# Attention over four images, one core: value work moved behind k and q, the small load moved to another queue

## The chip, the core and the metric

One core of a Trainium2 chip runs the whole kernel. It has a matrix engine (TensorE, in the profile PE, its weight loads PEld), a vector engine (VectorE, DVE), a scalar engine (ScalarE, ACT), GpSimd (POOL) and a queue engine (SyncE, SP), which here only issues loads and stores. Each engine runs its own instructions in order and waits on semaphores for the others. The metric is the device time of one execution in microseconds; the median over the runs counts.

## The reference

```python
q = jnp.einsum('oc,bcn->bon', Wq, xf) + bq[None, :, None]     # 32 x 1024 per image
k = jnp.einsum('oc,bcn->bon', Wk, xf) + bk[None, :, None]     # 32 x 1024
v = jnp.einsum('oc,bcn->bon', Wv, xf) + bv[None, :, None]     # 256 x 1024
scores = jnp.einsum('bqi,bqj->bij', q, k)                     # 1024 x 1024, no scaling
attn = jax.nn.softmax(scores, axis=-1)
out = jnp.einsum('bcj,bij->bci', v, attn)
return out.reshape(B, Cc, W, H) + x
```

There are four images of 256 channels and 32 x 32 = 1024 pixels, all in fp32.

## The kernel before

Every fp32 operand of a matrix product is held as two parts that TensorE takes at its fast rate: a *high* part (the number rounded to the type fp32r) and a *low* part (the rest). A product is then three matmuls: high by high, high by low, low by high. "Cutting" makes a high part, "splitting" the low part. The work of the other engines is mostly this, next to softmax.

An image runs through these steps. k and q are projected from the image (two halves of 512 pixels). Scores are made eight times 128 rows by 1024 columns; for each, VectorE takes the row maximum (`row_max`, L667) and ScalarE sums the exponentials of the row (`sum_exp`, L504). Then the scores are made once more, transposed and already shifted by the maximum (`scores_t`, L996: 128 keys by 512 pixels), ScalarE takes their exponential (`exp`, L539 and L542), which VectorE or POOL splits, and TensorE weighs the values with it (`weigh_v`, L1009 and L1015) into the banks `acc`. Values are eight tiles of 128 pixels by 256 channels (`v_tile`, L849: six matmuls each); two tiles share a bank, and a bank is cut by ScalarE or VectorE (`first_cut_v`) and split by VectorE (`split_v`, L715).

From image 1 on, a table (FRONT) lays the next image's steps between the weighting of the current one. Image 0 has nothing to hide behind: its beginning is an order written out by hand for each engine, and that is what the change rewrites. In it, the small load (`small_sb`: weights of k and q, biases) is issued by ScalarE, two loads of image 0 (one for each half of its channels), the value weights `wv` and image 1 by SP. TensorE runs twenty matmuls on zeros (`keep_busy`, L1076) until k and q can be projected (`first_project_qk`, L876 to L881). Of the 1024 pixels, q is put in three parts: pixels 0 to 255 (part 0), 256 to 511 (part 1) and the rest. For scores, `k_a` holds k high, k high again and k low, `q_a` holds a copy of q high (POOL's `put_q_dup`), q low (`put_q_lo`) and q high.

For image 0, only the first four scores (`first_scores` 0 to 3) are needed before the transposed scores of its first half; their row maxima are turned into rows by a small product with the identity (`first_rows`, L970), which ScalarE copies into `q_b` (`put_first_rows`, L514). Scores 3 use the bank of scores 0 again, so they wait until ScalarE has summed those (`rowsum_ready`). The banks of value tiles 0 to 3 are in `slot1`, those of tiles 4 to 7 in `slot0`, which scores 1 use before them. The weighting of key tile 0 waits for the split of the values it uses (`weigh_ready`, `v_split`).

## Time and profile before

| | us |
|---|---|
| median of 3 runs | 163.89 (163.86 to 164.11) |
| the profiled execution | 163.81 |
| its span in the trace | 162.0 |
| busy: TensorE, VectorE, ScalarE, POOL | 157.5, 133.9, 109.2, 60.0 |

The profile is of one execution. Its page gives busy times, the chain of work that ended last (followed back from the end, at each step to what released it), the costliest groups of instructions and the loads. The timeline shows single instructions with their start, their duration, and in brackets how long the engine had idled before and what ended that. A duration runs to the end of an instruction, and the next may start a little earlier, so of two equal ones the distance of the starts can be shorter than one duration. TensorE's ends are modelled. "Stretches" are tables of busy time between two times. The granted clock there is TensorE's as a share of full speed.

### The profile page before, as it was taken

The numbers are of one execution on the slowest core, as the hardware profiler recorded it, in microseconds if no ns is written. First come the engines' busy times: TensorE is split into PE (matmuls) and PEld (weight loads), VectorE is DVE, ScalarE is ACT, GpSimd is POOL, SyncE is SP. The second block draws the span as 40 slices with busy tenths as digits, with TensorE's granted clock in tenths as the row PEclk, the third lists the DMA queues.
The fourth block names the chain that finished last, engine by engine and source line by source line (L and its number), as shares of the span: only waits on it lengthen the run. The fifth ranks groups of instructions, "written<-read, shape, count | busy, mean of one in ns | idle before, by whom it ended". The sixth has DMA issues, their size and how long they took to land.

```text
span 162.0 us, 2456 instructions
## 1 busy us (share of the span) xinstructions
PE 157.5 (97%) x788; PEld 132.3 (82%) x788; DVE 133.9 (83%) x215; ACT 109.2 (67%) x200; POOL 60.0 (37%) x68
## 2 busy tenths in 40 slices
PE   7999999999999999999999999999999999999993
PEld 5677887798888887798888897788888898888882
DVE  1899998888988989997989989895989779846952
ACT  3679887969999545827999646736896655756400
POOL 4479946256222316348443300342333300124500
PEclk9999999999999999999999999999999999999999
DMA  4576672152103030162711130162320330003003
GB/s 161 187 299 166 243 235 89 31 151 63 55 0 97 1 129 2 37 144 67 268 39 49 54 129 0 37 146 67 121 61 1 97 129 0 0 5 129 0 0 130
DMA packets 7780, 14.67 MB, mean 91 GB/s; under 512 B 1504, under 2 KB 2072, under 8 KB 7768
## 3 DMA queue, kind: packets, MB, share of 16 engines
q1 hardware_dynamic: 6728, 13.46, 25.4%
q0 software_dynamic: 608, 0.80, 2.2%
q10 hardware_dynamic: 432, 0.26, 0.5%
q8 instruction: 6, 0.10, 0.3%
q14 instruction: 6, 0.05, 0.1%
HBM read 4.79 MB, written 4.20 MB: 55 GB/s over the span
## 4 chain that ended last, share of the span: by engine, by line
PE 90%; DMA 2%; ACT 2%; DVE 2%; issue 1%; DVEq 0%
PE acc L1009 32%; PE acc L1015 16%; PE slot L849 11%; PE st L996 9%; PE slot L909 7%; PE slot L1009 5%; DMA small_sb<-small 2%; PE slot L1015 2%; ACT dump L504 2%; PE slot L861 2%; PE slot L866 2%; PE slot L935 1%; DVE negmax L667 1%; PE slot L881 1%; DVE x_lo L632 0%
## 5 line engine op out<-in xcount | busy, mean ns | idle before, releaser
L402 POOL TENSOR_TENSOR w_lo<-w_full,w_hi 128x512 fp32r<-128x512 f32 x21 | 28.0, 1338 | 46.6 <-ACT w_full L542 25.4
L1009 PE MATMUL acc<-w_hi,v_hi 128*128 128x512 f32 x112 | 44.3, 395 | 0.0
L1009 PE MATMUL acc<-w_hi,v_lo 128*128 128x512 f32 x112 | 44.1, 394 | 0.0
L542 ACT ACTIVATE w_full<-st 128x512 f32<-128x512 f32 x62 | 36.8, 594 | 7.6 <-PE st L996 7.5
L504 ACT ACTIVATE dump<-slot,negmax 128x1024 f32<-128x1024 f32 x29 | 32.5, 1119 | 10.5 <-DVE negmax L667 10.1
L667 DVE TENSOR_REDUCE negmax<-slot 128x1 f32<-128x1024 f32 x29 | 35.2, 1217 | 2.7 <-PE slot L909 2.7
L1015 PE MATMUL acc<-w_lo,v_hi 128*128 128x512 f32 x112 | 37.4, 396 | 0.0
L734 DVE TENSOR_TENSOR w_lo<-w_full,w_hi 128x512 fp32r<-128x512 f32 x43 | 30.7, 719 | 3.6 <-issue 0.5
L1009 PEld LDWEIGHTS acc<-w_hi,v_hi 128*128 128x128 f32 x112 | 21.1, 189 | 5.0 <-issue 0.2
L1009 PEld LDWEIGHTS acc<-w_hi,v_lo 128*128 128x128 f32 x112 | 21.2, 189 | 4.8
L1015 PEld LDWEIGHTS acc<-w_lo,v_hi 128*128 128x128 f32 x112 | 21.0, 188 | 4.8
L996 PE MATMUL st<-q_b,k_b 98*128 98x512 f32 x62 | 24.5, 398 | 0.1
L725 DVE CAST w_hi<-w_full 128x512 fp32r<-128x512 f32 x40 | 19.5, 489 | 3.0 <-ACT w_full L542 1.5
L539 ACT ACTIVATE w_hi<-st 128x512 fp32r<-128x512 f32 x24 | 14.3, 594 | 6.2 <-PE st L996 6.0
L849 PE MATMUL slot<-wv_hi,x_hi 128*128 128x256 f32 x62 | 17.4, 281 | 0.4 <-ACT dump L504 0.4
L849 PE MATMUL slot<-wv_lo,x_hi 128*128 128x256 f32 x62 | 17.4, 281 | 0.0
L849 PE MATMUL slot<-wv_hi,x_lo 128*128 128x256 f32 x62 | 17.3, 280 | 0.0
L909 PE MATMUL slot<-k_a,q_a 96*128 96x512 f32 x48 | 15.2, 397 | 0.0
L531 ACT ACTIVATE v_hi<-slot 128x512 fp32r<-128x512 f32 x12 | 7.2, 599 | 11.8 <-PE slot L849 11.8
L265 POOL DMA_DIRECT2D q_b<-shift_rows x7 | 4.2, 602 | 29.5 <-DVE shift_rows L706 27.0
L715 DVE TENSOR_TENSOR v_lo<-slot,v_hi 128x512 fp32r<-128x512 f32 x16 | 11.0, 690 | 3.8 <-ACT v_hi L531 3.7
L909 PEld LDWEIGHTS slot<-k_a,q_a 96*128 96x128 f32 x48 | 13.0, 310 | 1.1
(102 smaller groups left out, 225.2 us busy)
## 6 DMA issues: line engine op xcount, KB each, us to landing
out<-x_sb SPq DMA_DIRECT2D x7, 512.0 KB, 2.8
x_sb<-x SPq DMA_DIRECT2D x3, 1024.0 KB, 5.1
k_b<-k_a SPq DMA_DIRECT2D x8, 192.0 KB, 2.6
q_b<-q_a SPq DMA_DIRECT2D x8, 192.0 KB, 2.6
x_sb<-x SPq DMA_DIRECT2D x2, 512.0 KB, 4.2
k_a<-qk_parts SPq DMA_DIRECT2D x12, 64.0 KB, 2.0
q_a<-qk_parts SPq DMA_DIRECT2D x12, 64.0 KB, 2.2
k_a<-qk_parts POOLq DMA_DIRECT2D x6, 64.0 KB, 2.2
```

The source lines that it names most:

```text
L402: nc.gpsimd.tensor_tensor(w_lo[:, r, :], w_full[:, r, :], w_hi[:, r, :].bitcast(fp32), ALU.subtract).then_inc(w_split_pool, 1)
L504: nc.scalar.activation(dump[:, t % 2, :], s_home(b, t), ACT.Exp, bias=negmax[:, t:t + 1], accum_out=rowsum[:, t:t + 1]).then_inc(rowsum_re ...
L539: nc.scalar.activation(w_hi[:, r, :], st_home(n), ACT.Exp).then_inc(w_cut_act, 1)
L542: nc.scalar.activation(w_full[:, r, :], st_home(n), ACT.Exp).then_inc(exp_done, 1)
L667: nc.vector.tensor_reduce(out=negmax[:, t:t + 1], in_=s_home(b, t), op=ALU.max, axis=AX.X, negate=True).then_inc(negmax_ready, 1)
L725: nc.vector.tensor_copy(w_hi[:, r, :], w_full[:, r, :]).then_inc(w_cut_dve, 1)
L734: nc.vector.tensor_tensor(w_lo[:, r, :], w_full[:, r, :], w_hi[:, r, :].bitcast(fp32), ALU.subtract).then_inc(w_split_dve, 1)
L849: last = nc.tensor.matmul(dst, lhs, rhs, start=(i == 0), stop=(i == len(terms) - 1))
L909: last = nc.tensor.matmul(s_home(b, t)[:, cols(h)], pixels(b, t), k_a[0:K_A, cols(h)], start=True, stop=True)
L996: nc.tensor.matmul(st_home(n), k_b[0:K_B, j * P:(j + 1) * P], q_b[0:K_B, cols(h)], start=True, stop=True).then_inc(st_ready, 1)
L1009: nc.tensor.matmul(dst, v[:, b % 2, j, c * P:(c + 1) * P], w_hi[:, n % RING, part], start=(j == 0 and v is v_hi), stop=False)
L1015: return nc.tensor.matmul(dst, v_hi[:, b % 2, j, c * P:(c + 1) * P], w_lo[:, n % RING, part], start=False, stop=(j == JT - 1))
```

## The change

- SP issues the small load, between the two loads of image 0, instead of ScalarE.
- VectorE splits the first quarter of image 0 (`x_lo`) before it makes the low part of the weights, and TensorE's first projection takes its three products in that order.
- q's first part is put by ScalarE (`put_q_hi(0)`), not VectorE; ScalarE alternates k and q and casts the value weights (`wv_hi`) only behind them. VectorE makes k low before q low.
- POOL copies the first q part before it builds the weight pairs for later images, the second before it splits the value weights; its cuts and splits of image 1 have other places among its first splits of weights.
- TensorE runs 18 warming matmuls, not 20, and 4 more behind the projection; first scores 0 come ahead of all values. Value tile 0 is made in two pieces (`first_v_high`, `first_v_low`), around scores 1 and 2; tile 1 follows, then scores 3, then tiles 2 and 3.
- ScalarE casts the first bank of values behind `put_first_rows`, not ahead of the sums. VectorE splits bank 1 before bank 0, and cuts bank 2 between them; the first weighting waits for two splits instead of one.

TensorE after the projection of k and q. Before, the rows are the last products of value tile 1 (L849), then scores 0, 1 and 2 (L935), then value tile 2:

```order
L849 MATMUL slot<-wv_hi,x_hi 128x256
L849 MATMUL slot<-wv_lo,x_hi 128x256
L849 MATMUL slot<-wv_hi,x_lo 128x256
L935 MATMUL acc<-k_a,q_a 128x512 [waits q_dup_put,q_lo_put,k_lo_put]
L935 MATMUL acc<-k_a,q_a 128x512 [waits k_lo_put]
L935 MATMUL slot<-k_a,q_a 128x512 [waits q_lo_put]
L935 MATMUL slot<-k_a,q_a 128x512
L935 MATMUL st<-k_a,q_a 128x512 [waits q_dup_put]
L935 MATMUL st<-k_a,q_a 128x512
L849 MATMUL slot<-wv_hi,x_hi 128x256 [waits q2_full_put]
```

and now (L1086 warming, L941 scores, L958 and L964 the two pieces of value tile 0):

```order
L1086 MATMUL st<-idle 128x256 x4
L941 MATMUL acc<-k_a,q_a 128x512 [waits q_dup_put,q_lo_put,k_lo_put]
L941 MATMUL acc<-k_a,q_a 128x512 [waits k_lo_put]
L958 MATMUL slot<-wv_hi,x_hi 128x256 [waits wv_cut]
L958 MATMUL slot<-wv_hi,x_lo 128x256
L958 MATMUL slot<-wv_hi,x_hi 128x256
L958 MATMUL slot<-wv_hi,x_lo 128x256
L941 MATMUL slot<-k_a,q_a 128x512 [waits q_lo_put]
L941 MATMUL slot<-k_a,q_a 128x512
L941 MATMUL st<-k_a,q_a 128x512 [waits q_dup_put]
L941 MATMUL st<-k_a,q_a 128x512
L964 MATMUL slot<-wv_lo,x_hi 128x256 [waits wv_split]
```

Value tiles 0 and 1 stood ahead of scores 0; now tile 0 lies around scores 1 and 2, and tile 1 follows the last row.

TensorE around scores 3 (into `acc`, waiting for the first sum). Before, the last products of value tile 3 stand ahead of it and tile 4 behind it:

```order
L849 MATMUL slot<-wv_hi,x_hi 128x256
L849 MATMUL slot<-wv_lo,x_hi 128x256
L849 MATMUL slot<-wv_hi,x_lo 128x256
L935 MATMUL acc<-k_a,q_a 128x512 [waits rowsum_ready]
L935 MATMUL acc<-k_a,q_a 128x512
L849 MATMUL slot<-wv_hi,x_hi 128x256 [waits rowsum_ready]
```

and now, where the row that waits for `q2_full_put` begins value tile 2:

```order
L850 MATMUL slot<-wv_hi,x_hi 128x256
L850 MATMUL slot<-wv_lo,x_hi 128x256
L850 MATMUL slot<-wv_hi,x_lo 128x256
L941 MATMUL acc<-k_a,q_a 128x512 [waits rowsum_ready]
L941 MATMUL acc<-k_a,q_a 128x512
L850 MATMUL slot<-wv_hi,x_hi 128x256 [waits q2_full_put]
L850 MATMUL slot<-wv_lo,x_hi 128x256
```

Two tiles (2 and 3) moved from before scores 3 to behind it; between scores 3 and the shift rows there are now four tiles, and there were two.

ScalarE from the cast of the value weights (L569) to the first exponential (L539), before:

```order
L569 ACTIVATE wv_hi<-wv 128x512 [waits wv_in]
L554 ACTIVATE k_a<-slot,small_sb 64x512 [waits qk_ready,small_in]
L554 ACTIVATE k_a<-slot,small_sb 64x512 [waits qk_ready]
L560 ACTIVATE q_a<-slot,small_sb 32x256 [waits q_lo_put]
L565 ACTIVATE qk_rest<-slot,small_sb 32x512 [waits qk_ready]
L523 ACTIVATE v_hi<-slot 128x512 [waits v_ready]
L504 ACTIVATE dump,rowsum<-acc,negmax 128x1024 [waits negmax_ready]
L504 ACTIVATE dump,rowsum<-slot,negmax 128x1024 [waits negmax_ready]
L504 ACTIVATE dump,rowsum<-st,negmax 128x1024 [waits rowsum_ready,negmax_ready]
L504 ACTIVATE dump,rowsum<-acc,negmax 128x1024 [waits rowsum_ready,negmax_ready]
L514 ACTIVATE q_b<-st 2x512 [waits row_ready]
L539 ACTIVATE w_hi<-st 128x512 [waits st_ready]
```

and now (L578 the value weights, L526 the first values):

```order
L557 ACTIVATE k_a<-slot,small_sb 64x512 [waits qk_ready,small_in]
L564 ACTIVATE q_a<-slot,small_sb 32x256
L557 ACTIVATE k_a<-slot,small_sb 64x512 [waits qk_ready]
L564 ACTIVATE q_a<-slot,small_sb 32x256 [waits q_lo_put]
L578 ACTIVATE wv_hi<-wv 128x512 [waits wv_in]
L569 ACTIVATE qk_rest<-slot,small_sb 32x512 [waits qk_ready]
L507 ACTIVATE dump,rowsum<-acc,negmax 128x1024 [waits negmax_ready]
L507 ACTIVATE dump,rowsum<-slot,negmax 128x1024 [waits negmax_ready]
L507 ACTIVATE dump,rowsum<-st,negmax 128x1024 [waits rowsum_ready,negmax_ready]
L507 ACTIVATE dump,rowsum<-acc,negmax 128x1024 [waits rowsum_ready,negmax_ready]
L517 ACTIVATE q_b<-st 2x512 [waits row_ready]
L526 ACTIVATE v_hi<-slot 128x512 [waits v_ready]
```

The value weights moved from ahead of k to behind q, the first values from ahead of the sums to behind the copy of the shift rows; q's first part came in.

The diff, cut to its core:

```diff
 (SP)
             for c in range(CT):
                 sp.dma_start(x_sb[:, 0, c, :], x_v[0, :, c, :]).then_inc(x0_in[c], DMA)
+                if c == 0:
+                    sp.dma_start(small_sb[:, :], small).then_inc(small_in, DMA)
 (POOL)
+            put_q_dup(0)
+            pool.wait_ge(q_dup_put, 1)
             for half, (parts, made) in enumerate(((wqk_hi, wqk_cut), (wqk_lo, wqk_split))):
...
             pool.wait_ge(pair_made, 2)
+            put_q_dup(1)
+            pool.wait_ge(q_dup_put, 2)
             pool.wait_ge(wv_cut, 1)
             nc.gpsimd.tensor_tensor(wv_lo[:, :, :], wv[:, :, :], wv_hi[:, :, :].bitcast(fp32),
                                     ALU.subtract).then_inc(wv_split, 1)
             pool.wait_ge(wv_split, 1)
-            put_q_dup(0)
-            pool.wait_ge(q_dup_put, 1)
-            put_q_dup(1)
-            pool.wait_ge(q_dup_put, 2)
...
+            pool.wait_ge(shift_ready, 1)
             cut_x1(1)
             split_x1(1)
             pool.wait_ge(x1_split, 2)
-            pool.wait_ge(shift_ready, 1)
             cut_x1(2)
+            pool.wait_ge(w_split_dve, SPLIT_COUNT[0])
             split_x1(2)
             pool.wait_ge(x1_split, 3)
+            split_w(1)
             cut_x1(3)
             pool.wait_ge(x1_cut, 4)
-            split_w(1)
 (ScalarE)
-            act.dma_start(small_sb[:, :], small).then_inc(small_in, DMA)
...
+            act.wait_ge(small_in, DMA)
+            put_k_hi(0)
+            put_q_hi(0)
+            put_k_hi(1)
+            put_q_hi(1)
             act.wait_ge(wv_in, DMA)
             nc.scalar.activation(wv_hi[:, :, :], wv[:, :, :], ACT.Copy).then_inc(wv_cut, 1)
-            act.wait_ge(small_in, DMA)
-            put_k_hi(0)
-            put_k_hi(1)
-            put_q_hi()
             put_q2_full()
-            first_cut_v(0)
             for t in range(TH):
                 sum_exp(0, t)
             put_first_rows()
+            first_cut_v(0)
             exp(0)
 (VectorE)
-            dve.wait_ge(qk_ready, 1)
-            nc.vector.tensor_scalar(out=q_a[2 * CQK:3 * CQK, Q_PARTS[0]], in0=q_home(0), ...
+            put_k_lo(0)
             put_q_lo(0)
-            put_k_lo(0)
             put_k_lo(1)
             put_q_lo(1)
             for t in range(TH):
                 row_max(0, t)
             first_shifts()
-            split_v(0, 0)
             first_cut_v(1)
             split_v(0, 1)
+            first_cut_v(2)
+            split_v(0, 0)
             invert_sums()
-            first_cut_v(2)
             split_v(0, 2)
 (TensorE)
+            def first_v_high():
+                pe.wait_ge(wv_cut, 1)
+                for c in range(CT):
+                    for xs in (x_hi, x_lo):
+                        nc.tensor.matmul(v_home(0, 0)[:, 0:C], xs[:, 0, c, 0:P], wv_hi[:, c, :], ...
+            def first_v_low():
+                pe.wait_ge(wv_split, 1)
+                for c in range(CT):
+                    nc.tensor.matmul(v_home(0, 0)[:, 0:C], x_hi[:, 0, c, 0:P], wv_lo[:, c, :], ...
...
-                    pe.wait_ge(v_split, 4 * b + 1 + j // VT)
+                    pe.wait_ge(v_split, 4 * b + 1 + j // VT if b + j else 2)
...
-            keep_busy(20, QUARTER)
+            keep_busy(18, QUARTER)
             for i in range(4):
                 first_project_qk(i)
-            pe.wait_ge(wv_cut, 1)
-            v_tile(0, 0)
-            v_tile(0, 1)
+            keep_busy(4, QUARTER)
             first_scores(0)
+            first_v_high()
             first_scores(1)
             first_scores(2)
+            first_v_low()
+            v_tile(0, 1)
+            first_scores(3)
             pe.wait_ge(q2_full_put, 1)
             v_tile(0, 2)
             v_tile(0, 3)
-            first_scores(3)
```

## Rows read from the trace of the kernel before

**Rows 1.** The page: busy time by engine; the last chain by engine.

```profile
PE 157.5 (97%) x788; PEld 132.3 (82%) x788; DVE 133.9 (83%) x215; ACT 109.2 (67%) x200; POOL 60.0 (37%) x68
...
PE 90%; DMA 2%; ACT 2%; DVE 2%; issue 1%; DVEq 0%
```

**Rows 2.** The chain of waits from 0 to 25 us: start, us, what.

```profile
0.75 3.94 DMA small_sb<-small
...
9.78 0.70 PE slot L849 x6
...
11.17 1.24 DVE negmax L667
...
17.05 0.59 ACT q_b L514
```

**Rows 3.** Timeline, 0 to 8 us: start, us, engine, line, operation, [idle before <- releaser].

```profile
0.74 0.86 SPq L278 DMA_DIRECT2D x_sb<-x  x2
...
4.50 1.15 ACT L490 ACTIVATE x_hi<-x_sb 128x512 fp32r<-128x512 f32 x2 [2.04 <-DMA x_sb<-x]
4.71 0.29 DVE L624 CAST wqk_hi<-small_sb 128x256 fp32r<-128x256 f32 x1 [3.43 <-DMA small_sb<-small]
5.04 0.43 DVE L626 TENSOR_TENSOR wqk_lo<-small_sb,wqk_hi 128x256 fp32r<-128x256 f32 x1
...
5.38 2.68 DVE L632 TENSOR_TENSOR x_lo<-x_sb,x_hi 128x512 fp32r<-128x512 f32 x4
...
7.72 0.39 PE L881 MATMUL slot<-x_lo,wqk_hi 128*128 128x512 f32 x1
```

**Rows 4.** Stretches: from:to, us, busy by engine, granted clock, load share, GB/s.

```profile
2.00:3.00 1.00, 1.00 (x7) 0.69 (x6) 0.00 (x0) 0.46 (x1) 0.84 (x1) 1.00 0.54 176
3.00:4.00 1.00, 1.00 (x6) 0.71 (x5) 0.00 (x0) 0.00 (x0) 0.00 (x0) 1.00 1.06 410
...
24.00:160.00 136.00, 135.22 (x675) 114.92 (x673) 114.84 (x185) 91.74 (x171) 43.92 (x44) 1.00 0.22 69
```

**Rows 5.** Timeline, 8 to 11 us: VectorE and ScalarE on k and q.

```profile
8.15 0.48 DVE L769 TENSOR_SCALAR q_a<-slot,small_sb 32x256 fp32r<-32x256 f32 x1
...
8.21 1.31 ACT L554 ACTIVATE k_a<-slot,small_sb 64x512 fp32r<-64x512 f32 x2 [0.72 <-PE slot L881]
...
9.18 1.40 DVE L642 SCALAR_TENSOR_TENSOR k_a<-slot,small_sb,k_a 32x512 fp32r<-32x512 f32 x2
```

**Rows 6.** Timeline, 13 to 17 us: TensorE's scores 3 and shift rows.

```profile
13.69 0.74 PE L935 MATMUL acc<-k_a,q_a 96*128 96x512 f32 x2
...
16.41 0.40 PE L970 MATMUL st<-eye_r,shift_parts 128*2 128x128 f32 x4
```

**Rows 7.** Timeline, 10 to 24 us: casts and splits of values, exponentials, weighting.

```profile
10.62 0.60 ACT L523 ACTIVATE v_hi<-slot 128x512 fp32r<-128x512 f32 x1
...
18.23 0.60 ACT L539 ACTIVATE w_hi<-st 128x512 fp32r<-128x512 f32 x1 [0.59 <-PE st L996]
...
18.92 0.69 DVE L715 TENSOR_TENSOR v_lo<-slot,v_hi 128x512 fp32r<-128x512 f32 x1
...
18.97 0.47 PE L1009 MATMUL acc<-w_hi,v_hi 128*128 128x512 f32 x1
...
21.98 1.11 ACT L504 ACTIVATE dump<-slot,negmax 128x1024 f32<-128x1024 f32 x1
...
23.24 0.54 PEld L935 LDWEIGHTS slot<-k_a,q_a 96*128 96x128 f32 x2 [0.27 <-ACT dump L504]
```

**Rows 8.** Timeline, 7 to 22 us: POOL's subtractions.

```profile
7.64 1.58 POOL L424 TENSOR_TENSOR wv_lo<-wv,wv_hi 128x512 fp32r<-128x512 f32 x1 [1.34 <-ACT wv_hi L569]
...
12.09 1.28 POOL L384 TENSOR_TENSOR q_a<-qk_rest,q_a 32x512 fp32r<-32x512 f32 x1
...
20.92 1.29 POOL L402 TENSOR_TENSOR w_lo<-w_full,w_hi 128x512 fp32r<-128x512 f32 x1 [0.23 <-ACT w_full L542]
```

**Rows 9.** Timeline of TensorE alone, 3.5 to 4.5 us: warming matmuls.

```profile
3.17 1.70 PE L1076 MATMUL st<-idle 128*128 128x256 bf16 x7
```

More of the change, by code:

```diff
@@ L766, in finish @@
                                                scalar=bv_sb[:, c:c + 1], in1=x_sb[:, b, c, cols(h)], op0=ALU.add, op1=ALU.add).then_inc(acc_read, 1)
-            dve.wait_ge(qk_ready, 1)
-            nc.vector.tensor_scalar(out=q_a[2 * CQK:3 * CQK, Q_PARTS[0]], in0=q_home(0),
-                                    scalar1=bias[2 * CQK:3 * CQK, 0:1], scalar2=None,
-                                    op0=ALU.add).then_inc(q_hi_put, 1)
+            put_k_lo(0)
             put_q_lo(0)
-            put_k_lo(0)
             put_k_lo(1)
@@ L877, in first_project_qk @@
                 if i == 0:
+                    pe.wait_ge(x0_split, 1)
+                    nc.tensor.matmul(dst, wqk_hi[:, c, :], x_lo[:, 0, c, part], start=False, stop=False)
                     pe.wait_ge(wqk_split, 1)
+                    nc.tensor.matmul(dst, wqk_lo[:, c, :], x_hi[:, 0, c, part], start=False, stop=False)
+                    return
                 nc.tensor.matmul(dst, wqk_lo[:, c, :], x_hi[:, 0, c, part], start=False, stop=False)
```

27 lines of the change are left out of this document (12 added, 15 removed).

## The prediction

> **What bounds the kernel now.** I read the page first: TensorE is busy for 97% of the span and carries 90% of the chain that ended last [rows 1]. The stretch from 24 to 160 us is 136.0 us long and TensorE is busy in 135.2 of them [rows 4]. Nothing is won or given back there: what the first 24 us gain or lose reaches the end whole. The change touches only those 24 us, so the chain of that stretch is the next view [rows 2]. It is no TensorE chain at first: the small load lands at 4.69, weights and image 0 are cut, k and q are made, VectorE takes the first row maximum at 11.17, ScalarE runs four sums of exponentials, copies the shift rows at 17.05, and only then come transposed scores, exponentials and the weighting (18.97 in [rows 7]). Values and POOL's splits have room beside this chain; the question for each edit is whether it shortens the chain or eats that room.
>
> **The change part by part.** *Loads and weight cut.* The small load moves behind the first half of image 0 on SP's queue. Before, ScalarE starts to cut that half at 4.50, VectorE the weights at 4.71 [rows 3]. The load is 128 x 132 x 4 = 68 KB, 0.16 us at the 410 GB/s of the stretch from 3 to 4 us [rows 4]; so much sooner may the half land. VectorE's instructions stay (0.29, 0.43, four x low of 2.68 / 4 = 0.67), only the first x low goes ahead of the weights' low part. With the old landings it starts at 4.50 + 0.62 = 5.12 (one cut is 0.62, since two take 1.15 overlapped), and the third ends at 5.12 + 0.67 + 0.43 + 2 x 0.67 = 7.56; before it ended at about 7.4 and TensorE, slightly behind, ended the first half of k and q at 7.72 + 0.39 = 8.11 [rows 3]. After it can end near 8.1, with the 0.16 nearer to 7.95. I take **-0.1**. No row shows a small load behind another on SP's queue, so the bounds are wide: +0.2 and -1.0 (rivals below). The two dropped warming matmuls end before the weights are there and cost nothing.
>
> The Trainium skill (Trainium Kernel Development and Optimization, Key Constraints) says that loads issued by SP, ScalarE and GpSimd run on the same engines and interleave, and that issuing from several only saves issue time. By that rule the move buys no bandwidth, and the small load waits for SP's issue of the half ahead of it; that is the second rival, and the trace of before can't decide it.
>
> *k and q.* Before, VectorE made q high, q low, k low, k low: from 8.15 to 10.58 (the last row, 9.18 + 1.40) [rows 5]. Now ScalarE makes q high and VectorE waits for k high first: 8.21 + 0.68 (half of the pair's 1.31, and a little) = 8.89, then k low 0.66 (spacing within that pair of 1.40), q low 0.48 (as long as q high), k low 0.74 with small gaps: 10.83. That is +0.25, and with the -0.1 above **+0.15** for the second half of the first scores and so for the first row maximum (11.17 becomes 11.32). ScalarE's part hides: its second k high ends at about 9.9, before VectorE wants it at 10.1.
>
> *Values behind k and q.* Value weights are cast at about 10.5 to 11.1 instead of 6.9, and TensorE's queue holds the first value products between scores 0 and scores 1. Scores 1 then end near 12.2, and the second row maximum wants them at 11.32 + 1.13 = 12.45: covered by 0.2. POOL does the weight pairs and both q copies first, then the values' low part, which took 1.58 at 7.64 but of which a like subtraction took 1.28 at 12.09 [rows 8]. It ends between 12.4 and 13.1, and TensorE does tile 1 of the values behind it, 0.7 us [rows 2]. Scores 3 can't start before the first sum has freed its bank, 13.69 + 0.15 = 13.84 [rows 6], so a low part that ends by 12.9 costs nothing; I take 1.28 and no cost, and 0.2 as the upper bound.
>
> The Trainium skill (GPSIMD Engine Reference, 1. Specifications) says that POOL shares its SBUF interfaces with VectorE and contends with VectorE's instructions of two SBUF inputs. The rows agree: 1.58 stands beside the x low subtractions, 1.28 beside row maxima out of PSUM. By the rule the low part takes 1.28 in its new place and the sum stays; with 1.58 it would be 0 to 0.2 higher.
>
> *Scores 3.* Here is the price. Before, value tiles 2 and 3 ran ahead of scores 3, in its wait. Now tile 1 stands there and tiles 2 and 3 behind it. From 13.84 TensorE has scores 3 (two matmuls, 0.47), four value tiles at 0.70 [rows 2] and the shift rows: these start at 13.84 + 0.47 + 2.80 = 17.11 instead of 16.41, and take 0.40 [rows 6], so ScalarE may copy at 17.5. ScalarE's own sums would let it copy at 17.05 + 0.15 = 17.20. Before, TensorE was 17.05 - 16.81 = 0.24 early; now it is last, by 0.3. The copy comes **+0.5** late, of which 0.15 is the k and q step.
>
> *First values in ScalarE's wait.* The copy takes 0.59, the transposed scores follow, and before ScalarE idled 0.59 in front of the first exponential [rows 7]; the cast of the first values is 0.60, so it fits and costs at most 0.05. But VectorE can split these values only then: copy done at 18.1, cast done at 18.75, split (0.69) done at 19.45 [rows 7]. The weighting now waits for two splits; it would start at 18.97 + 0.5 = 19.47 anyway. A tie, and no cost.
>
> *VectorE behind that split.* The third split, 18.92 before [rows 7], comes after the reciprocal at 19.5, **+0.6** instead of +0.5; behind it stand, in the old order, the first weights' low part, the last split and the row maximum of scores 4. The exponential of scores 4 at 21.98 goes to 22.6 with it, and TensorE already waited 0.27 us for the end of that one at 23.24 [rows 7]. So the next point at which TensorE waited moves by 0.6 and not by 0.5. POOL's first low part of weights (20.92, 1.29) [rows 8] now stands behind a third x low and ends near 23.4; TensorE wants it at about 23.3. That wait lies inside the 0.6, with 0.3 as the upper bound.
>
> **Sum.** -0.1 + 0.25 + 0.35 (scores 3) + 0.1 (VectorE behind the late split) = **+0.6 us**. The profiled execution took 163.81, so 164.41; it stands 0.08 under the median of 163.89, so the forecast is 164.5. With the bounds of the unknown costs (-0.3 for better landings, +0.4 for POOL and for a small load that lands later) the forecast's own range is 164.2 to 164.9.
>
> **Rivals.** *Earlier loads, and faster.* In the stretch from 2 to 3 us the load engines moved 176 GB/s against 410 in the next [rows 4]. Were the fault ScalarE's load among the first rows, image 0 could land up to (410 - 176) / 410 = 0.57 sooner, and at the most 1.0 with a shorter way from last byte to wait. A gain of 0.6 is needed to balance, 0.95 to come out faster by over 0.2%. At 1.0 in place of my 0.1 the time is 164.5 - 0.9 = 163.6. For it speaks the slow stretch; against it that 410 is reached with both queues at work, and that the second half's landing at about 5.8 would have to move too. Faster 0.07; the milder form, 0.3 to 0.95 sooner, gives 163.7 to 164.2: 0.15.
>
> *Small load later.* Two issues of SP take 0.86 [rows 3]. If the small load lands later by one of them, at 5.1, VectorE starts its chain there: 5.1 + 0.3 + 0.67 + 0.43 + 1.34 = 7.85, k and q end near 8.4 in place of 8.0, and the first weights cost 0.3 to 0.4: 164.8. The long landing of before (3.9 us for 68 KB) speaks for a load that waits its turn. 0.09.
>
> *TensorE falls to its lower clock.* The warming matmuls of 256 columns come at seven in 1.70 us [rows 9], some 0.21 apart once the last one's own tail is taken off, the level of 1.2 GHz; a value tile's six in 0.70 [rows 2], 0.117 apart, that of 2.4. The granted clock's column reads 1.00 even in the slow stretch [rows 4], so the spacing tells it. Between the projection and scores 3 the new order leaves holes (about 0.9, 0.5 and 0.3 us) where before value tiles stood. If the clock fell there, five tiles would take 3.5 us more, of which at most 0.5 is covered; with a quick return about half, 166 to 167.5. Against it: four new warming matmuls, and no hole above 1 us. 0.05.
>
> The Trainium skill (TensorE: Matmul & The Clock Gate, Part 1) says that the low clock is the default and that recent activity releases it; no run so far shows a fall in this kernel.
>
> **Chances.** Forecast 0.64, later small load 0.09, low clock 0.05: slower by over 0.2% (0.33 us, about what a measurement of this kernel can tell from no change) 0.78. Within it 0.15, faster 0.07. The range takes in the milder loads and the later small load, and leaves most of the clock and of the faster case out: 163.8 to 165.1.
>
> **What would show it.** In the profile after: first row maximum near 11.3; shift rows (TensorE into st, 128 columns) at 17.1, and ScalarE's copy released by them and not by its own last sum; VectorE idle for some 0.5 us ahead of the split of the first values; the weighting at 19.5; TensorE's wait for the exponential of scores 4 ending near 23.9. It is wrong if the first row maximum comes before 10.8 (loads), if POOL's low part of the value weights ends after 13.2, or if value tiles take over 1 us each (clock).

## The result

The changed kernel takes 165.94 us at the median of 6 runs (165.49 to 166.80), the kernel before 163.88 (163.71 to 164.11): ratio 1.0129, 95% interval 1.011 to 1.0148, so **slower by 2.06 us**, where the prediction had +0.6 and a range up to 165.1. The profiled execution of after took 165.96 with a span of 164.2 (before 163.81 and 162.0). Two single executions of later kernels, 312.65 (e13) and 221.19 (e17), lie far above all others, and the ratios, unlike the medians, leave them out. The page of after, busy times and last chain, against [rows 1]:

```profile
PE 158.8 (97%) x790; PEld 132.5 (81%) x790; DVE 135.0 (82%) x214; ACT 109.8 (67%) x201; POOL 58.5 (36%) x68
...
PE 96%; DVE 2%; ACT 0%; issue 0%; DVEq 0%; ACTq 0%
```

The chain is now 96% TensorE's (90% before): behind the first scores nearly nothing else stands between two steps. The busy times say little; where the time went is read in the order of time. Timeline of after, 0 to 8 us, against [rows 3]; last a row of before:

```profile
1.19 0.42 SPq L281 DMA_DIRECT2D small_sb<-small  x1
1.65 0.43 SPq L278 DMA_DIRECT2D x_sb<-x  x1
...
4.19 1.15 ACT L493 ACTIVATE x_hi<-x_sb 128x512 fp32r<-128x512 f32 x2 [2.16 <-DMA x_sb<-x]
4.37 0.29 DVE L629 CAST wqk_hi<-small_sb 128x256 fp32r<-128x256 f32 x1 [3.09 <-DMA small_sb<-small]
...
6.92 1.16 ACT L493 ACTIVATE x_hi<-x_sb 128x512 fp32r<-128x512 f32 x2 [1.58 <-DMA x_sb<-x]
```

```profile
5.82 1.15 ACT L490 ACTIVATE x_hi<-x_sb 128x512 fp32r<-128x512 f32 x2 [0.17 <-DMA x_sb<-x]
```

The first half of image 0 and the weights land 0.3 earlier, as the prediction's -0.1 wanted. The second half lands at 6.92, where it was 5.82, and ScalarE stands idle for 1.58. Stretches of after (from:to, us, busy by engine, granted clock, load share, GB/s):

```profile
3.00:4.00 1.00, 1.00 (x6) 0.71 (x5) 0.00 (x0) 0.00 (x0) 0.00 (x0) 1.00 0.87 247
4.00:5.00 1.00, 1.00 (x7) 0.52 (x4) 0.44 (x2) 0.81 (x2) 0.00 (x0) 1.00 0.75 148
```

Before, the stretch from 3 to 4 moved 410 GB/s [rows 4], the next 408; now the load engines are busy for 0.87 and 0.75 of two stretches and move 247 and 148. Then k, q and the first scores, 8 to 13 us, against [rows 5]:

```profile
8.94 0.68 ACT L557 ACTIVATE k_a<-slot,small_sb 64x512 fp32r<-64x512 f32 x1 [0.86 <-PE slot L887]
...
9.64 0.46 ACT L564 ACTIVATE q_a<-slot,small_sb 32x256 fp32r<-32x256 f32 x1
...
11.01 0.47 PE L941 MATMUL acc<-k_a,q_a 96*128 96x512 f32 x1 [1.02 <-DVE q_a L653]
...
12.27 1.23 DVE L672 TENSOR_REDUCE negmax<-acc 128x1 f32<-128x1024 f32 x1
```

The first row maximum is at 12.27 instead of 11.17: 0.73 is there at the first k high (8.94 against 8.21), 0.37 comes in k and q. Then the shift rows, 16 to 20 us, against [rows 6, 7]:

```profile
16.95 1.30 POOL L415 TENSOR_TENSOR x_lo<-x_sb,x_hi 128x512 fp32r<-128x512 f32 x1
17.00 1.28 DVE L679 CAST shift_parts<-negmax 128x4 fp32r<-128x4 f32 x1
...
18.58 0.40 PE L979 MATMUL st<-eye_r,shift_parts 128*2 128x128 f32 x4 [0.23 <-issue]
...
19.02 0.59 ACT L517 ACTIVATE q_b<-st 2x512 fp32r<-2x512 f32 x1 [0.89 <-PE st L979]
```

VectorE's cast of 128 x 4 numbers takes 1.28 us (0.20 in the kernel before): it stands beside POOL's first subtraction on image 1, which began at 14.12 before, and ends with it. Shift rows and copy come 2.17 and 1.97 late. The weighting starts at 21.05 (18.97 before). Last, TensorE at 25 to 28 us in after, and the first scores behind 25 us in before:

```profile
25.05 0.30 PEld L1025 LDWEIGHTS acc<-w_lo,v_hi 128*128 128x128 f32 x2 [0.41 <-POOL w_lo L405]
...
27.73 0.63 PE L941 MATMUL slot<-k_a,q_a 96*128 96x512 f32 x2
```

```profile
25.55 0.63 PE L935 MATMUL slot<-k_a,q_a 96*128 96x512 f32 x2
```

From scores 7 (27.73, before 25.55: +2.18) on, the lateness stays as it is to the end (+2.2 in the span).

### The profile page after: what moved, and what is told of

It is laid out like the page before. It is cut to its first block, busy times and chain, and to the rows that moved or that the text cites. A ratio compares the mean times of both kernels' runs of the same rounds, so it can differ in the third digit from the quotient of the medians.

```text
span 164.2 us, 2462 instructions
## 1 busy us (share of the span) xinstructions
PE 158.8 (97%) x790; PEld 132.5 (81%) x790; DVE 135.0 (82%) x214; ACT 109.8 (67%) x201; POOL 58.5 (36%) x68
## 4 chain that ended last, share of the span: by engine, by line
PE 96%; DVE 2%; ACT 0%; issue 0%; DVEq 0%; ACTq 0%
PE acc L1019 32%; PE acc L1025 16%; PE slot L850 13%; PE st L1005 9%; PE slot L915 7%; PE slot L1019 5%; PE st L1086 2%; PE slot L1025 2%; PE slot L862 2%; PE slot L867 2%; PE slot L941 1%; DVE k_a L647 1%; PE slot L877 1%; PE acc L941 1%; PE slot L887 0%; ACT k_a L557 0%
```

## The experiments

Each begins at the kernel before or after; medians in us, ratio to the kernel before, measured beside it, with its 95% interval. This table is worked out from the timelines of the profiled executions; "scores 7" are the fourth scores behind the start of the weighting, the last point at which kernels differ. A profiled execution need not be the median one: that of e2 took 165.07.

| kernel | median | first row maximum | weighting | scores 7 | scores 7 less row maximum |
|---|---|---|---|---|---|
| before | 163.88 | 11.17 | 18.97 | 25.55 | 14.38 |
| after | 165.94 | 12.27 | 21.05 | 27.73 | 15.46 |
| e2: before + the load's move | 164.61 | 11.30 | 19.97 | 26.77 | 15.47 |
| e4: loads back, POOL apart | 165.07 | 11.51 | 19.85 | 26.71 | 15.20 |
| e9: e4 + POOL's weights first | 165.11 | 11.56 | 19.88 | 26.67 | 15.11 |
| e10: e4 + values ahead | 165.07 | 11.73 | 19.59 | 26.75 | 15.02 |
| e13: e4 + both | 164.60 | 11.75 | 19.62 | 26.17 | 14.42 |
| e14: e13 + k and q back | 164.22 | 11.38 | 19.25 | 25.82 | 14.44 |
| e17: e14 with 20 warming matmuls | 164.16 | 11.37 | 19.24 | 25.80 | 14.43 |
| e16: e4 + k and q back, tile 5 moved | 164.73 | 11.15 | 19.23 | 26.28 | 15.13 |
| e18: before + k and q | 164.56 | 11.61 | 19.50 | 26.30 | 14.69 |

### The loads

**e1: after, small load back on ScalarE.**

```diff
                 sp.dma_start(x_sb[:, 0, c, :], x_v[0, :, c, :]).then_inc(x0_in[c], DMA)
-                if c == 0:
-                    sp.dma_start(small_sb[:, :], small).then_inc(small_in, DMA)
 (ScalarE)
+            act.dma_start(small_sb[:, :], small).then_inc(small_in, DMA)
```

> The changed kernel with the small load back on ScalarE's queue; nothing else is undone. Theory A (the small load between the two halves makes the second half of image 0 land at 6.92 instead of 5.82): the half lands near 5.8 again, the first row maximum comes 0.8 to 1.1 us earlier than in the changed kernel, the time is 164.7 to 165.2. Theory B (the new order of k, q and values costs the 2 us, the landing is hidden): within 0.3 us of the changed kernel, 165.6 to 166.2.

165.36, ratio 1.0096 (1.0073 to 1.0119): 0.58 is given back, a little less than theory A wanted. The second half is back at 5.76, the first row maximum at 11.52, 0.75 ahead of after. The profiled execution is one of 166.01, in which TensorE's clock fell (below), so its rows behind 12 us can't be compared.

**e2: before, with the load's move alone** (the + and - of e1 the other way round).

> The kernel before with only the small load moved to SP's queue between the two halves. Theory A: the second half lands near 6.9, k and q end 0.6 to 0.7 us later, the time is 164.5 to 164.9. Theory B: the first half and the weights land 0.3 us earlier and the time stays at 163.6 to 164.1.

164.61, ratio 1.006 (1.0033 to 1.0086): slower by 0.7, as theory A had it, but not in its way. In the profiled execution (165.07) the half landed at 6.28, and the first row maximum is only 0.13 late (11.30). What follows is a collision: the subtraction that makes the shift's low part met POOL's. Timelines of before and of e2, 16 to 17 us:

```profile
16.14 0.17 DVE L676 TENSOR_TENSOR shift_parts<-negmax,shift_parts 128x4 fp32r<-128x4 f32 x1
16.16 1.31 POOL L412 TENSOR_TENSOR x_lo<-x_sb,x_hi 128x512 fp32r<-128x512 f32 x1
```

```profile
16.22 1.27 POOL L415 TENSOR_TENSOR x_lo<-x_sb,x_hi 128x512 fp32r<-128x512 f32 x1
16.23 1.28 DVE L678 TENSOR_TENSOR shift_parts<-negmax,shift_parts 128x4 fp32r<-128x4 f32 x1
```

Before, VectorE begins 0.02 ahead of POOL and takes 0.17; in e2 it begins 0.01 behind and takes 1.28. The shift rows then come at 17.61 instead of 16.41. How much of the median's 0.7 is landing and how much is this collision, no profile of a median execution shows.

**e3: after, second half issued by ScalarE**, SP issuing the first half, the small load, wv.

> The changed kernel, but ScalarE issues the second half of image 0 while SP issues the first half, the small load and the value weights. If the late half is a matter of its place behind the small load on one queue, it lands by 5.8 or earlier, with the first half still near 4.2 and the small load near 4.4: 164.5 to 165.0. If the load engines share their time and the queue is no matter, the first half and the small load land later too and the time is 165.0 to 165.9.

167.33, ratio 1.0196 (1.0155 to 1.0236), slower than after and than either theory gave. The first half lands at 5.46, later than in any other kernel here, the second by 5.65 (0.74 and 4.9 from issue to landing), and the small load at 5.85: from another queue the second half runs beside the first and takes its time. In two of the four executions the clock shows 0.99 too.

**e5: before, second half only issued later.**

```diff
             for c in range(CT):
+                if c:
+                    sp.wait_ge(eye_cut, 1)
                 sp.dma_start(x_sb[:, 0, c, :], x_v[0, :, c, :]).then_inc(x0_in[c], DMA)
```

> The kernel before, with nothing moved between queues: SP only holds the issue of image 0's second half until POOL has made the identity, about 0.7 us (one and a half issues of SP at 0.45) later than before, and wv behind it. Theory 'issue': the half lands late because it is issued late; by as much, so near 6.3 to 6.6 instead of 5.82, the first row maximum 0.4 to 0.7 later than 11.17, and the time 164.4 to 164.8. Theory 'rows': the half was late because the small load's many short rows stood ahead of it in the same queue; with those on ScalarE's queue a late issue costs little, the half lands by 6.0, and the time stays within 164.2.

163.85, ratio 1.0003 (0.9994 to 1.0012): nothing lost. The half lands at 5.76 all the same. So it is not the issue, 0.46 later in after, that makes it late.

**e6: before, small load first on SP; e15: before, small load last, behind both halves.**

```diff
 (e6)
+            sp.dma_start(small_sb[:, :], small).then_inc(small_in, DMA)
             for c in range(CT):
                 sp.dma_start(x_sb[:, 0, c, :], x_v[0, :, c, :]).then_inc(x0_in[c], DMA)
 (e15)
             for c in range(CT):
                 sp.dma_start(x_sb[:, 0, c, :], x_v[0, :, c, :]).then_inc(x0_in[c], DMA)
+            sp.dma_start(small_sb[:, :], small).then_inc(small_in, DMA)
```

> The kernel before with the small load issued by SP ahead of both halves of image 0, not by ScalarE. Theory 'issue': each half is issued one issue (0.45) later; the weights land earlier and are cut before image 0 is there, which gives VectorE back at most 0.3 to 0.4; first k high near 8.2 to 8.4, time 163.8 to 164.3. Theory 'rows': everything behind the short rows is late, both halves by 0.7 to 1.1, and the time is 164.6 to 165.0. If the small load among the first rows were what made the stretch from 2 to 3 us slow, as my prediction's fast rival had it, the halves would land earlier and the time would be under 163.6.

> The kernel before with the small load issued by SP behind both halves of image 0. Theory 'place': only a half that is issued behind the small load in the same queue, with the other half ahead of it, is late; here both halves land as before (4.2 to 4.5, 5.8), and the weights, issued at 1.65 instead of 0.75, land near 5.0 to 5.6, which starts VectorE's weight cut 0.3 to 0.9 later: 164.2 to 164.8, from the weights, not from image 0. Rival 'queue': the small load on SP's queue delays the second half wherever it stands in it; half at 6.3 or later.

In both, ScalarE's own issue of it is gone. e6: 164.01 (163.64 to 165.09), ratio 1.0019 (0.9998 to 1.0041), not to be told from before. e15: 165.83, ratio 1.0114 (1.0099 to 1.0129). Timelines of e6 and of e15, 2 to 9 us:

```profile
2.63 0.36 DVE L624 CAST wqk_hi<-small_sb 128x256 fp32r<-128x256 f32 x1 [1.35 <-DMA small_sb<-small]
...
4.67 2.45 ACT L490 ACTIVATE x_hi<-x_sb 128x512 fp32r<-128x512 f32 x4 [2.63 <-DMA x_sb<-x]
```

```profile
4.00 1.15 ACT L490 ACTIVATE x_hi<-x_sb 128x512 fp32r<-128x512 f32 x2 [1.97 <-DMA x_sb<-x]
5.30 1.15 ACT L490 ACTIVATE x_hi<-x_sb 128x512 fp32r<-128x512 f32 x2 [0.15 <-DMA x_sb<-x]
5.54 0.29 DVE L624 CAST wqk_hi<-small_sb 128x256 fp32r<-128x256 f32 x1 [4.26 <-DMA small_sb<-small]
...
6.21 3.77 DVE L632 TENSOR_TENSOR x_lo<-x_sb,x_hi 128x512 fp32r<-128x512 f32 x4
...
7.22 1.61 POOL L425 TENSOR_TENSOR wv_lo<-wv,wv_hi 128x512 fp32r<-128x512 f32 x1
```

With the small load first or last, the second half follows the first as it did before (in e6 four cuts run in one piece). Only in the place between them is the second half late. Theory 'place' holds for the loads, and 'rows' falls. The load isn't free elsewhere: with it last, both halves land 0.5 earlier than before (4.00 and 5.30), with it first, the first half 0.17 later. e15 misses its time, though: 0.83 later weights cost 1.9, because VectorE's four subtractions, 2.68 before [rows 3], take 3.77 around POOL's of 1.61: the late chain ran into the value weights' subtraction, which began at 7.64 before, beside the last x low alone [rows 8].

### VectorE behind POOL

**e4: e1, with POOL's first subtraction of image 1 held until the shift is out.**

```diff
             cut_x1(0)
+            pool.wait_ge(shift_ready, 1)
             split_x1(0)
             pool.wait_ge(x1_split, 1)
-            pool.wait_ge(shift_ready, 1)
             cut_x1(1)
```

> The kernel of e1 (small load on ScalarE's queue) with POOL's first subtraction on image 1 held until VectorE has made the shift parts. Theory C (VectorE's 128x4 cast, 1.28 us in the changed kernel against 0.20 before, waits for POOL's two-input subtraction): the cast takes 0.2, and since TensorE's value tiles end 0.4 us ahead of the shift rows, the time falls by 0.2 to 0.4 us below e1. Rival (the cast is slow for another reason, or TensorE's tiles end last anyway): within 0.15 us of e1.

165.07, ratio 1.0073 (1.0057 to 1.0089): 0.29 less than e1, measured with it, though the intervals overlap. VectorE's two small instructions take 0.17 each, where the cast took 1.28 in after. (They take 0.17 in e1's profile too: with its low clock the shift came later, at the end of POOL's subtraction.) The profiles to compare are after and e4: scores 7 less row maximum go from 15.46 to 15.20. But the copy still waits for the shift rows. Timeline of e4, 17 to 25 us:

```profile
17.43 0.40 PE L976 MATMUL st<-eye_r,shift_parts 128*2 128x128 f32 x4
...
17.86 0.58 ACT L514 ACTIVATE q_b<-st 2x512 fp32r<-2x512 f32 x1 [0.49 <-PE st L976]
...
24.04 0.30 PEld L1022 LDWEIGHTS acc<-w_lo,v_hi 128*128 128x128 f32 x2 [0.55 <-POOL w_lo L402]
```

That is the scores 3 term as predicted (four value tiles in front of the shift rows), and POOL's late first low part of weights. From scores 3 (14.03) to the weighting (19.85) TensorE's matmuls follow one another without a gap that the profile marks.

### k and q

**e8: e4 with the old order of k and q; e18: before with the new one.** Edit of e18 (e8 is its reverse):

```diff
 (ScalarE)
             put_k_hi(0)
+            put_q_hi(0)
             put_k_hi(1)
-            put_q_hi()
+            put_q_hi(1)
 (VectorE)
-            nc.vector.tensor_scalar(out=q_a[2 * CQK:3 * CQK, Q_PARTS[0]], in0=q_home(0), ...
-            put_q_lo(0)
-            put_k_lo(0)
+            put_k_lo(0)
+            put_q_lo(0)
             put_k_lo(1)
             put_q_lo(1)
```

> As e4_pool_apart (165.07), with only k and q in the old order: VectorE makes q's first part high itself, while ScalarE makes k high. First row maximum near 11.2 instead of 11.51. If the row maxima set the end, or TensorE's hole ahead of scores 0 does, 0.25 to 0.35 is won: 164.7 to 164.85. If the four value tiles behind scores 3 set it alone, with TensorE waiting for nothing that k and q give, nothing is won: 165.0 to 165.1.

> The kernel before with the change's order of k and q alone: ScalarE makes k high, q high, k high, q high, and VectorE k low, q low, k low, q low. My prediction gave this +0.25; the profiles of e4, e8 and e14 read 0.35 to 0.45, since ScalarE's first q high now stands ahead of its second k high, for which VectorE's second k low waits. First row maximum near 11.5 and 164.2 to 164.35 by the profiles; 11.4 and 164.05 to 164.15 by my prediction.

e8: 164.63 (164.59 to 166.3), ratio 1.0066 (1.0038 to 1.0093), 0.44 under e4 by the medians. Its profiled execution, 164.99, shows little: its first three products start 0.64 and 0.60 apart, where those of e4 start 0.64 and 0.33 apart, and its first row maximum is at 11.48. e18: 164.56, ratio 1.0033 (1.0019 to 1.0048), above both ranges. Timeline of e18, 8 to 17 us:

```profile
8.27 0.68 ACT L554 ACTIVATE k_a<-slot,small_sb 64x512 fp32r<-64x512 f32 x1 [0.71 <-PE slot L879]
...
8.98 0.47 ACT L561 ACTIVATE q_a<-slot,small_sb 32x256 fp32r<-32x256 f32 x1
...
9.47 0.68 ACT L554 ACTIVATE k_a<-slot,small_sb 64x512 fp32r<-64x512 f32 x1
...
10.27 0.74 DVE L644 SCALAR_TENSOR_TENSOR k_a<-slot,small_sb,k_a 32x512 fp32r<-32x512 f32 x1
...
16.20 0.61 POOL L408 CAST x_hi<-x_sb 128x512 fp32r<-128x512 f32 x1
16.34 0.50 DVE L676 CAST shift_parts<-negmax 128x4 fp32r<-128x4 f32 x1
```

ScalarE's pair of k highs is cut in two by q high: the second starts 1.20 behind the first, and VectorE's second k low waits for it until 10.27. First row maximum 11.61, +0.44, of which 0.06 is a later landing: **+0.38**. The rest of e18's +0.66 is the cast of the shift, 0.50 instead of 0.20: everything behind k and q now falls 0.4 later, and the cast beside a cast of POOL's (16.20 to 16.81), with which it ends, in a kernel whose POOL order is the old one.

### Values and POOL's weights

**e9: e4, POOL's first weights ahead of its third split; e16: e8, value tile 5 behind the shift rows.**

```diff
 (e9)
             pool.wait_ge(w_split_dve, SPLIT_COUNT[0])
+            split_w(1)
             split_x1(2)
             pool.wait_ge(x1_split, 3)
-            split_w(1)
 (e16)
             v_tile(0, 4)
-            v_tile(0, 5)
             pe.wait_ge(rowsum_ready, 3)
             first_rows()
+            v_tile(0, 5)
```

> As e4_pool_apart (165.07), but POOL makes the low part of weights 1 ahead of its third split of image 1, not behind it, so it starts near 21.3 instead of 22.70. Theory 'POOL': TensorE waited for it at 24.04 (0.55 on its weight loads, 0.3 to 0.4 on its matmuls), so 0.3 to 0.5 is won: 164.6 to 164.8. Rival: the wait covers another that ends as late (VectorE's splits or the exponential of scores 4), and nothing is won: 165.0 to 165.1.

> As e8_kq_back (164.63), with value tile 5 behind the shift rows instead of ahead of them, so three value tiles stand between scores 3 and the shift rows. My prediction's term 'scores 3' has the copy of the shift rows as what counts: shift rows near 16.75 instead of 17.40, the copy 0.4 to 0.5 earlier, time 164.2 to 164.35. Theory 'TensorE full': from scores 3 to the weighting TensorE has no idle time left, so the copy comes earlier, the value tiles stand behind it, the weighting starts within 0.1 of 19.83, and the time stays at 164.55 to 164.7.

e9: 165.11, ratio 1.0091 (1.0056 to 1.0126): nothing won, though the wait for POOL is gone; scores 7 start as in e4. In its place TensorE waits 0.31 at 24.34 for the exponential of scores 4, the wait that the prediction had named (near 23.9). e16: 164.73, ratio 1.0046 (1.0031 to 1.0061): nothing won either. Timeline of e16, 16 to 24 us:

```profile
17.03 0.59 ACT L514 ACTIVATE q_b<-st 2x512 fp32r<-2x512 f32 x1
...
18.05 0.63 PE L1005 MATMUL st<-q_b,k_b 98*128 98x512 f32 x2
...
23.61 0.30 PEld L1025 LDWEIGHTS acc<-w_lo,v_hi 128*128 128x128 f32 x2 [0.85 <-POOL w_lo L402]
```

The copy is early now and waits for nothing, but TensorE makes two value tiles before it comes to the transposed scores (18.05, 0.43 behind the copy's end), and 0.85 is then lost at POOL. The weighting at 19.23 is 0.6 earlier than e16's own expectation gave; 0.33 of that is an earlier first row maximum (11.15), the other 0.27 is a gain that is taken back at POOL. So e16 doesn't show what the copy's place is worth without that wait: with e9's order of POOL it was not run.

**e7: e4, values ahead of scores 0 again; e10: the same with 24 warming matmuls; e13: e10 and e9's edit.** Edit of e7 on TensorE (ScalarE casts wv ahead of k, POOL makes its low part ahead of the q copies; e10 has keep_busy(24) for 18):

```diff
-            keep_busy(4, QUARTER)
-            first_scores(0)
             first_v_high()
-            first_scores(1)
-            first_scores(2)
             first_v_low()
             v_tile(0, 1)
-            first_scores(3)
+            first_scores(0)
+            first_scores(1)
+            first_scores(2)
             pe.wait_ge(q2_full_put, 1)
             v_tile(0, 2)
             v_tile(0, 3)
+            first_scores(3)
```

> As e4_pool_apart (small load on ScalarE, POOL's split apart; 165.07), but value tiles 0 and 1 stand ahead of scores 0 again: ScalarE casts the value weights ahead of k, POOL makes their low part first, TensorE makes tiles 2 and 3 ahead of scores 3; k and q, the cast of the first values and POOL's order of weights stay as after. Theory 'hole': moving 1.4 us of value work out of the time in which TensorE waits for k and q, to behind scores 0, is what costs, since TensorE has no slack left from scores 0 on; giving it back gives 0.5 to 0.9, so 164.2 to 164.6. Rival 'k and q': the first row maximum sets the end, and stays at 11.5; the time stays at 164.8 to 165.1.

> As e7_values_back (166.6), with 24 warming matmuls ahead of the projection instead of 18. In the profile of e7 TensorE idled 0.34 between the last warming matmul and the first product, and then ran the projection's products 0.43 apart (1.2 GHz) until 10.1; the other kernels' rise came at 5.5 to 6.7. Theory 'warming': the two warming matmuls that the change drops can leave that hole, and the clock then rises late; without the hole products are 0.23 apart from 6.7 at the latest, and values ahead of scores 0 give what e7 was to give: 164.2 to 164.7. Rival: the late rise has another cause, and 166.6 stays.

> As e10_values_back_warm (165.07), with POOL's low part of weights 1 ahead of its third split of image 1, as in e9. In e10 the weighting starts at 19.59, 0.62 later than before against 0.88 in e4, but TensorE then waits 0.94 for POOL at 24.10 and both kernels end alike. If that wait hides what values ahead of scores 0 give back, 0.4 to 0.6 is won here, where e9 won nothing: 164.5 to 164.7. If values ahead of scores 0 are worth nothing, 165.0 to 165.1.

e7: 166.60 (165.13 to 166.67), ratio 1.0146 (1.0104 to 1.0188), and it can't be read for the values: TensorE ran nearly the whole projection at its lower clock (one of four executions, 165.13, was quicker). Timelines of TensorE in e7 and in e10:

```profile
5.42 0.76 PE L874 MATMUL slot<-x_hi,wqk_hi 128*128 128x512 f32 x1 [0.34 <-ACT x_hi L490]
...
9.71 0.63 PE L874 MATMUL slot<-x_hi,wqk_hi 128*128 128x512 f32 x1
10.14 0.51 PE L882 MATMUL slot<-x_hi,wqk_lo 128*128 128x512 f32 x1
```

```profile
6.73 0.40 PE L874 MATMUL slot<-x_hi,wqk_hi 128*128 128x512 f32 x1
6.96 0.39 PE L882 MATMUL slot<-x_hi,wqk_lo 128*128 128x512 f32 x1
```

Products stand 0.43 apart until 10.14 in e7 (1.2 GHz), 0.23 in e10 (2.4 GHz). e10: 165.07, ratio 1.0088 (1.0066 to 1.0109), outside both its ranges. Its weighting starts 0.26 ahead of e4's, but TensorE then waits 0.94 for POOL, and both reach scores 7 alike. e13: 164.60, ratio 1.0046 (1.003 to 1.0062): with both edits 0.47 is won by the median, and scores 7 less row maximum go from 15.20 to 14.42, where e9 alone had 15.11 and e10 alone 15.02. (The median gives less, 0.47 for 0.78, since e13's first row maximum is 0.24 later than e4's; e17 shows why.) **Two limits of the same lateness stood side by side**: TensorE's value work without a hole to stand in, and POOL's first weights behind a third split. Either edit alone uncovers the other.

**e14: e13 with k and q back; e17: e14 with 20 warming matmuls.**

> As e13_values_pool, with k and q in the old order too (VectorE makes q's first part high). What is left of the change is the order of the x splits, the place of the first values' cast, and POOL's order around the row shift. If loads, POOL's collision, k and q, and value work moved behind scores 0 are the whole loss, this is the kernel before to within 0.3: 163.9 to 164.2. If something else of the change costs, 164.3 or more.

> As e14_values_pool_kq (164.22), with 20 warming matmuls ahead of the projection, as in the kernel before, instead of 24. In e14 the 24 ran until 5.71, beyond the point (5.3) where the first product could start, and the first row maximum came at 11.38 instead of 11.17. If those four extra matmuls are what is left of the loss, 163.9 to 164.05 here; if another part of the change is, 164.15 to 164.3.

e14: 164.22, ratio 1.0021 (1.001 to 1.0032), 0.38 under e13, measured with it, which is the price of k and q again. e17: 164.16, ratio 1.0015 (1.0005 to 1.0024): the four warming matmuls are not what is left. Timelines of e17 and of e4, 4 to 8 us:

```profile
4.56 1.15 ACT L490 ACTIVATE x_hi<-x_sb 128x512 fp32r<-128x512 f32 x2 [2.10 <-DMA x_sb<-x]
...
5.18 0.29 POOL L418 CAST wqk_pair<-wqk_hi 128x128 fp32r<-128x128 f32 x1 [2.34 <-DVE wqk_hi L625]
...
5.22 0.80 DVE L633 TENSOR_TENSOR x_lo<-x_sb,x_hi 128x512 fp32r<-128x512 f32 x1 [0.18 <-ACT x_hi L490]
...
6.28 1.98 DVE L633 TENSOR_TENSOR x_lo<-x_sb,x_hi 128x512 fp32r<-128x512 f32 x3
...
6.42 0.69 POOL L418 CAST wqk_pair<-wqk_lo 128x128 fp32r<-128x128 f32 x1 [0.94 <-DVE wqk_lo L630]
```

```profile
4.43 1.15 ACT L490 ACTIVATE x_hi<-x_sb 128x512 fp32r<-128x512 f32 x2 [1.97 <-DMA x_sb<-x]
...
5.09 0.69 DVE L634 TENSOR_TENSOR x_lo<-x_sb,x_hi 128x512 fp32r<-128x512 f32 x1
...
6.04 1.89 DVE L634 TENSOR_TENSOR x_lo<-x_sb,x_hi 128x512 fp32r<-128x512 f32 x3
```

From the landing of the first half to the end of the four x lows it is 3.70 in e17 (4.56 to 8.26), 3.56 in before and 3.55 in e18 (both the old order), and 3.50 in e4, which has the new order too. So the new order of the first split costs nothing by itself. In e17, as in e7, e10, e13 and e14, POOL builds the weight pairs and the value weights' low part beside the x lows again, in after and e4 only behind them; with the new order these meet more of them. By these rows 0.14 of e17's later first row maximum (11.37, before 11.17) come from mixing the two kernels and not from the change; 0.06 are a later landing, and the weighting adds 0.07.

### The clock

**e11: after with 14 warming matmuls behind the projection, not 4.**

> The kernel after with 14 warming matmuls behind the projection instead of 4 (10 more at 0.12 each, as long as the hole of 1.0 in which TensorE waits for k and q). Theory 'clock': one execution in six of the kernel after showed a clock of 0.99, and e1's profile shows it fall to half from 12.4 to 15.6, 1.6 us behind such a hole; with the hole filled no execution shows less than 0.995, the spread goes below 0.4, and the median goes down by 0.1 to 0.4, to 165.5 to 165.8. Rival: the median is set by the late half of image 0, k and q, and POOL alone, and stays at 165.8 to 166.0 with the clock of every execution at 1.0; the warming matmuls may then cost up to 0.2 where they run on past k and q.

165.92 (165.78 to 166.03), ratio 1.0128 (1.0112 to 1.0144): the median is the same, so the clock is not in it. Without the filled hole single executions do pay: e1's profiled one (166.01, the other three 165.26 to 165.44); with it, no one of four does. Stretches of e1:

```profile
12.00:13.00 1.00, 1.00 (x4) 0.80 (x4) 0.90 (x2) 0.24 (x2) 0.94 (x2) 0.58 0.35 90
13.00:14.00 1.00, 1.00 (x5) 0.87 (x4) 1.00 (x2) 0.98 (x2) 0.94 (x2) 0.50 0.85 256
...
15.00:16.00 1.00, 1.00 (x6) 0.86 (x6) 0.20 (x1) 1.00 (x3) 0.94 (x2) 0.71 0.00 0
```

The granted clock (third column from the end) falls to half in the stretch from 12 to 13 and is back in that from 15 to 16, behind a hole of 1.03 at 10.26 in which TensorE waited for q. e4's profile has the same hole (1.02 at 10.25) and no fall, so the hole alone doesn't decide it.

**e12: e6 with 24 warming matmuls**, the one try at a kernel faster than before.

> As e6_small_first (the kernel before with the small load first on SP's queue; 163.64 to 163.72 in four of ten executions, 163.97 to 165.09 in six), with 24 warming matmuls instead of 20. In e6 TensorE idled 0.4 ahead of the first product. If that hole lets the clock rise late in some executions, all now come at 163.6 to 163.8, a little ahead of the kernel before (163.84); if the spread comes from where the loads land, it stays, with a median of 163.9 to 164.1.

164.00 (163.59 to 164.40), ratio 1.001 (0.9997 to 1.0023): the spread is smaller (0.81, in e6 1.45) and doesn't go, so it is not the warming alone, and no version here beats the kernel before.

## Why the prediction was wrong

**Right**: that the first 24 us decide; the direction; the mechanism at scores 3 (four value tiles, shift rows late, copy released by TensorE, as e4 shows it); the first values' cast in ScalarE's wait, which cost some 0.1 (the weighting starts 1.39 behind the first transposed scores, 1.28 before); POOL's low part of the value weights at 1.28 (1.29 measured). But its own signs came late: first row maximum 12.27 for 11.3, shift rows 18.58 for 17.1, weighting 21.05 for 19.5.

**Loads and weight cut, taken at -0.1 with bounds of +0.2 and -1.0: the step that failed.** It cost 0.58 by the medians (e1), 0.73 at the first k high of the profiles. The first half and the weights did land 0.3 earlier; the working then carried "the old landings" of the second half over, and no term asked what a load in the middle of a queue does to the one behind it: the second half landed 1.10 later. The prediction's rival of a later small load looked at the wrong load. The upper bound of 0.2 had no row behind it. The new order of the first split was rightly taken as a gain of some hundredths (3.50 in e4, 3.56 before).

The Trainium skill (DMA: Bandwidth & Descriptors, Issuing engines are not separate DMA queues) says that loads from all engines run on the same 16 DMA engines and interleave, and that issuing from several saves only issue time. By that rule alone the move would cost issue time, and e5 shows that a later issue is worth nothing here; yet between two loads of SP's the small load delayed the second by 0.46 in e2 and by 1.10 in after. The measurement decides.

**k and q, taken at +0.25: +0.38** (e18; e13 to e14). The working let ScalarE's second k high end at 9.9; with q high between, it started 0.49 after q high, and VectorE's second k low waited for it. "ScalarE's part hides" was wrong.

**POOL beside VectorE: not in the sum at all.** The prediction weighed POOL's shared interface for the value weights alone. The loss (0.26 by the profiles of after and e4, 0.29 by the medians of e1 and e4) came where POOL's first split of image 1, which starts at 16.95 instead of 14.12, meets the two smallest instructions of the chain. The Trainium skill (SBUF — State Buffer, Who interferes with whom) says that VectorE and GpSimd share a pair of ports as an exclusive lock: whoever issues first has it for its whole instruction, and the other stands still. The traces agree: an instruction on 128 x 4 numbers took 1.28 behind a subtraction of 1.30 (after) and of 1.27 (e2), 0.50 up to the end of a cast of POOL's (e18), and 0.17 alone (e4) or begun 0.02 ahead of POOL (before). So a delay of a tenth can cost a whole microsecond, or nothing.

**Scores 3 at +0.35, VectorE behind it at +0.1, POOL's first weights "inside the 0.6": together some 0.76** (15.20 to 14.44 in the table). The copy of the shift rows was the right place to look, but not the only limit: e16 made it wait for nothing, started the weighting 0.27 earlier for it, and lost that again at POOL. From scores 3 on TensorE's queue is full (e4), since 1.4 us of value work had left the time in which it waits for k and q; e13 shows this and POOL's weights together. And POOL's wait, held to lie inside, is a second limit of the same size.

**The sum** by the profiled executions, at scores 7: 0.73 at the first k high (loads), 0.37 k and q, 0.26 POOL beside VectorE, 0.76 values with POOL's weights, 0.06 left: 2.18. Of the 1.58 by which this is above +0.6, the loads are 0.83, values with POOL's weights 0.31, POOL beside VectorE 0.26, k and q 0.12. By medians, undone in this order: 0.58 (e1), 0.29 (e4), 0.47 (e13), 0.38 (e14), 0.06 (e17), 0.26 left; there the undoing itself moves POOL's work beside the x lows. Left open is why the second half is late, and why by 1.10 in after and by 0.46 in e2, with the same loads in the same order: runs show the place, not the cause.

**The clock rival** (0.05) took place in single executions; in e1's it cost 0.57 to 0.75 (166.01 against 165.26 to 165.44). It was no part of the median (e11).

## What to carry to other kernels

Before a load is moved within a queue, ask of each load behind it when it lands, and give that its own bound. A move by 0.1 us of a whole stretch (e2) can push a tiny instruction of one engine behind a long one of another that shares its port, so list what each moved instruction will stand beside, and how far it is from it. When an edit that removes a visible wait wins nothing, look for a second limit of the same lateness, and remove both before judging either.

## What was not expected of the hardware

- A load of 68 KB between two of 512 KB on one queue: the second landed at 6.28 (e2) and 6.92 (after), not 5.82; first or last in the queue it did not (e6: first half at 4.67, four cuts in one piece; e15: halves at 4.00 and 5.30). In after the load engines were busy for 0.75 of the stretch from 4 to 5 and moved 148 GB/s, in e2 for 0.93 and moved 364.
- The small load landed 1.9 us behind its issue when first (0.74 to 2.63), and 3.9 when last (1.64 to 5.54).
- Two instructions that begin 0.02 apart: VectorE's on 128 x 4 numbers took 0.17 when it began ahead of POOL's subtraction (before), 1.28 when it began behind it (e2).
- In e7 the products ran 0.43 apart, the level of 1.2 GHz, until 10.14, after 0.34 of idling behind the warming matmuls; e4 idled 0.57 there and ran on at 0.23, so the hole alone doesn't decide it. The granted clock's column reads 1.00 in e7's projection as in e10's, so the spacing has to be read too.
